# Second half of an attention and expert-layer kernel: new hand-written orders, chunk 0 normalised by VectorE, group scores from pair sums, both table reads ahead of the weight loads

## The chip, the cores and the metric

The kernel runs on one core of one Trainium2 chip. The metric is device microseconds (us) for one execution. The kernel before takes 311.48 us, the median of three runs (310.99 to 311.97).

Engines by the profile's names: PE is TensorE's matmul, PEld its weight load, DVE is VectorE, ACT ScalarE, POOL GpSimd, SP SyncE. SP only starts DMAs. Each engine works through its own list of instructions in order and waits on semaphores, so an instruction that waits holds up all that is behind it on its engine.

## The reference, cut to what matters

```
x = x + L0_xattn(layernorm(x), ctx)     # one head over 32 keys: softmax(qk)v, (x_norm + attended) Wo
x = x + L0_ffn(layernorm(x))            # 8 experts, top 1, gelu
x = x + L1_xattn(layernorm(x), ctx)     # 16 heads of 8 channels
x = x + L1_ffn(layernorm(x))            # 16 experts of 96, top 4, and one shared expert
```

`x` is (4, 512, 128). The routing of the last layer:

```
scores = sigmoid(x @ gate_w.T); sb = scores + gate_bias
group_scores = sum of the two largest sb in each of 4 groups of 4 experts
keep the 2 best groups, then the 4 best experts in them; w = 2.5 * score / sum
y = sum over experts of w * (silu(x w1) * (x w3)) w2 + shared expert
```

## The kernel before, in words

The 2048 tokens are four chunks (0 to 3) of 512, each of 4 tiles of 128 tokens. The first half (first attention, first expert layer) ends by writing its results to DRAM in sorted order. The second half fetches them back token by token (`fetch`, 16 indirect DMAs that POOL issues), adds them to `x` (`combine`), and does the second attention and the last expert layer.

The second half is one list of stages per engine, `ORDER1`, written out by hand, each entry `stage:number`. Up to `gturn` and the routing, numbers are chunks. For `g`, `u`, `e`, `prod`, `hm`, `high`, `low`, `silu` and `y` they are tiles of work: 52 of them, 13 a chunk, 12 routed row blocks (16 experts of 96 rows are 12 blocks of 128) and one shared.

A chunk's attention runs: statistics (DVE), `rstd2` (POOL: `ve`, `nm`, a power to `rstd`, a product to `shift_of`, lines 770 to 775), `norm2` (ACT, `normalise`, line 581), `turn2` (PE transposes, 1178), `unturn2` (ACT copy, 586), `q` (PE), `qcopy` (ACT), `score` (PE), `max` (DVE, four reductions of one bank each, 1037), `mturn` (PE transposes, 1373), `mcopy` (ACT), `scoreT` (PE), `exp` (ACT), `zav` (PE: sums into bank 4, products into bank 5), `div` (DVE: two reciprocals, 1045, 3.4 us together, then two products, 1051), `wo` (PE), `add` (DVE, 1056, with the statistics of the next normalisation). Then `rstd3`, `norm3`, `turn3`, `unturn3`, `round` (ACT: high half of x), `lowx` (POOL: low half, 779), `logit` (PE), `lgcopy` and `sg` (ACT), `route0` to `route7` (DVE, 30-odd short instructions that each wait for the one before), `gturn` (PE transposes of the gates, 1414) and `gcopy` (ACT).

A tile of expert work runs: `g` and `u` (PE, three matmuls of 512 columns each), `silu` (ACT), `prod` (DVE, 1143), `e` (PE, one matmul that spreads the gates), `hm` (DVE, 1154), `high` (ACT, 746), `low` (POOL, 854), `y` (PE, three matmuls). `g` writes bank 0, `u` bank 1, `e` bank 3, one buffer each: `g:n` waits for `silu:n-1`, `u:n` for `prod:n-1`, `e` for the `hm` before it.

`FILL` puts matmuls that compute nothing, of 512 bfloat16 columns, ahead of a chunk-0 stage on PE.

In the first expert layer SP reads two small tables into registers: which expert each of 23 token tiles has (`tile_e`) and where its tokens lie (`tile_r`). It reads the first, starts the first five weight loads, reads the second, waits for the scatter of the tokens and for the zero padding, and starts the token loads.

## Time and profile before

| | us |
|---|---|
| median of three runs | 311.48 |
| the profiled execution | 313.38 |
| its span, first to last instruction | 311.6 |
| PE busy | 264.1 (85%) |
| DVE busy | 191.7 (62%) |
| ACT busy | 162.9 (52%) |
| POOL busy | 155.4 (50%) |

An engine's busy time is the sum of its instructions' durations. Matmul records overlap a little, so PE can look full. The granted clock of PE over the span is 0.919 of full speed; it is at half (1.2 of 2.4 GHz) in three stretches of the windows asked for, 26 to 36 us, 40 to 70 us and 108 to 114 us, and at or near full from 70 to 107 us and from 115 us on.

By the profile's timeline the second half begins at 98.5 us with the first fetch; chunk 0's `turn2` starts at 109.67, the first expert tile (`g:0`) at 143.87 and the last `y` at 306.11.

### The profile page before, as it was taken

The page shows a single profiled execution, that of the slowest core. Times are in us where ns is not written, and L with a number is a line of the kernel's source. Part 1 is how long each engine was busy: PE and PEld are TensorE (multiplying, and loading weights), DVE is VectorE, ACT ScalarE, POOL GpSimd, SP SyncE. Part 2 cuts the span into 40 slices and gives each one's busy share as a digit, 9 for nine tenths or more (in the row PEclk, how much of TensorE's full clock was granted, in tenths as well). Part 3 has the DMA queues.
Part 4 walks back from the last instruction along what each step waited for, and adds up shares of the span by engine and source line. Part 5 has one row for each costly group of instructions (what it writes and reads, how often), then busy time and mean ns, then how long its engine had stood idle before and what let it go on. Part 6 is the DMA issues. An engine that isn't in the chain of part 4 may idle for free. (4 is left out here: it accounts for less than half of the span.)

```text
span 311.6 us, 4963 instructions
## 1 busy us (share of the span) xinstructions
PE 264.1 (85%) x1542; PEld 193.6 (62%) x1542; DVE 191.7 (62%) x577; ACT 162.9 (52%) x324; POOL 155.4 (50%) x182
## 2 busy tenths in 40 slices
PE   8899962259989287979899987999899989899993
PEld 7689852249984042444468645875477867687871
DVE  5555557014441348666975998689976599665561
ACT  2946330485641034157488654878457745455541
POOL 6722577439402888251176151743178535565561
PEclk9996655559999969999999999999999999999998
DMA  7960013447841111000000000000000000000000
GB/s 239 405 236 1 18 35 101 119 127 191 241 130 37 51 35 34 8 2 0 2 0 2 1 0 1 2 0 14 23 1 0 2 34 1 1 2 34 0 0 34
DMA packets 15372, 16.86 MB, mean 54 GB/s; under 512 B 2147, under 2 KB 13011, under 8 KB 15091
## 3 DMA queue, kind: packets, MB, share of 16 engines
q1 hardware_dynamic: 9520, 11.65, 11.8%
q10 hardware_dynamic: 4802, 2.80, 2.9%
q0 software_dynamic: 1024, 2.10, 2.4%
q8 instruction: 12, 0.20, 0.3%
q14 instruction: 14, 0.11, 0.1%
HBM read 11.96 MB, written 4.59 MB: 53 GB/s over the span
## 5 line engine op out<-in xcount | busy, mean ns | idle before, releaser
L854 POOL TENSOR_TENSOR lring<-hm,hring 128x512 fp32r<-128x512 f32 (+1 forms) x52 | 67.9, 1307 | 77.6 <-ACT hring L746 76.3
L740 ACT ACTIVATE act<-bank 128x512 f32<-128x512 f32 (+1 forms) x52 | 31.0, 597 | 38.5 <-PE bank L1166 38.3
L1143 DVE TENSOR_TENSOR act<-act,bank 128x512 f32<-128x512 f32 x48 | 32.9, 685 | 27.0 <-PE bank L1166 25.7
L1166 PE MATMUL bank<-xTh,gu1h 128*128 128x512 f32 (+1 forms) x104 | 43.6, 419 | 2.6 <-DVE hm L1154 1.7
L1166 PE MATMUL bank<-xTh,gu1l 128*128 128x512 f32 (+1 forms) x104 | 41.1, 395 | 0.0
L1166 PE MATMUL bank<-xTl,gu1h 128*128 128x512 f32 (+1 forms) x104 | 40.8, 393 | 0.0
L581 ACT ACTIVATE xn<-x,shift_of,rstd 128x128 f32<-128x128 f32 x64 | 26.4, 483 | 26.4 <-POOL shift_of L775 26.3
L1154 DVE TENSOR_TENSOR hm<-act,bank 128x512 f32<-128x512 f32 (+1 forms) x52 | 35.6, 685 | 7.4 <-PE bank L1166 4.9
L746 ACT CAST hring<-hm 128x512 fp32r<-128x512 f32 (+1 forms) x52 | 32.1, 618 | 12.4 <-DVE hm L1154 11.4
L1166 PEld LDWEIGHTS bank<-xTh,gu1h 128*128 128x128 f32 (+1 forms) x104 | 19.3, 186 | 14.8 <-DVE act L1143 3.6
L788 POOL DMA_INDIRECT xn<-sorted_y,home x16 | 15.7, 983 | 21.2 <-DMA sorted_y<-ys 17.3
L1166 PE MATMUL bank<-hring,w2h 128*128 128x512 f32 (+1 forms) x52 | 21.6, 414 | 1.7 <-POOL lring L854 1.7
L1166 PEld LDWEIGHTS bank<-xTh,gu1l 128*128 128x128 f32 (+1 forms) x104 | 19.3, 186 | 4.8
L1166 PE MATMUL bank<-warm_b,onesb 128*128 128x512 bf16 x87 | 21.2, 391 | 0.5 <-issue 0.5
L1166 PEld LDWEIGHTS bank<-xTl,gu1h 128*128 128x128 f32 (+1 forms) x104 | 19.4, 186 | 3.3
L1178 PE MATMUL bank<-pack_a,xn 128*128 128x128 f32 x64 | 12.8, 315 | 9.3 <-ACT xn L581 8.1
L1166 PE MATMUL bank<-lring,w2h 128*128 128x512 f32 (+1 forms) x52 | 20.5, 395 | 0.0
L1166 PE MATMUL bank<-hring,w2l 128*128 128x512 f32 (+1 forms) x52 | 20.5, 395 | 0.0
L1166 PE MATMUL bank<-gT,sel 128*128 128x512 f32 x48 | 19.9, 414 | 0.6 <-DVE hm L1154 0.6
L682 ACT ACTIVATE hT<-bank,w 128x128 f32<-128x128 f32 x46 | 14.4, 364 | 10.5 <-PE bank L1166 10.5
L784 POOL DMA_INDIRECT sorted_x<-xn,slot x16 | 15.8, 985 | 4.6 <-issue 4.6
L586 ACT COPY xT<-bank 128x512 f32<-128x512 f32 x16 | 9.4, 584 | 16.0 <-PE bank L1178 13.2
(217 smaller groups left out, 521.0 us busy)
## 6 DMA issues: line engine op xcount, KB each, us to landing
w<-in_w SPq DMA_DIRECT2D x23, 129.0 KB, 2.4
wf<-in_gu SPq DMA_DIRECT2D x1, 1632.0 KB, 14.2
xs<-sorted_x SPq DMA_DIRECT2D x23, 64.0 KB, 2.5
sorted_y<-ys ACTq DMA_DIRECT2D x11, 128.0 KB, 3.1
x<-in_x SPq DMA_DIRECT2D x4, 256.0 KB, 5.1
w<-in_w SPq DMA_DIRECT2D x1, 1024.0 KB, 9.6
out_x<-x SPq DMA_DIRECT2D x4, 256.0 KB, 2.0
w<-in_w SPq DMA_DIRECT2D x1, 768.0 KB, 14.9
```

The costliest lines, as they stand in the source:

```text
L581: nc.scalar.activation(normal(k, b)[:, j, :], x[:, b * TPB + j, :], ACT.Identity, bias=shift_of[:, ln(k, b), j:j + 1], scale=rstd[:, ln(k, ...
L586: nc.scalar.copy(xT[:, xT_slot(k, b), :], bank[n][:, :]).then_inc(s.xT_ready[k], 1)
L682: last = nc.scalar.activation(hT0[:, t % 2, k, :], bank[2 + t % 2][:, k * P:(k + 1) * P], ACT.Gelu, bias=b1_tile[:, t % SLOTS0, k:k + 1])
L740: nc.scalar.activation(act[0:m, n % 4, :], bank[0][0:m, :], ACT.Silu).then_inc(s.act_ready1, 1)
L746: nc.scalar.copy(hring[0:m, n % 4, :], hm[0:m, n % 4, :]).then_inc(s.hmh_ready, 1)
L784: nc.gpsimd.indirect_dma_start(xs_dram[:, :], bass.IndirectOffsetOnAxis(ap=slot0[:, t:t + 1], axis=0), xn2[:, t, :], None).then_inc(s.scat ...
L788: nc.gpsimd.indirect_dma_start(xn2[:, t, :], None, ys_dram[:, :], bass.IndirectOffsetOnAxis(ap=home0[:, t:t + 1], axis=0))\
L854: nc.gpsimd.tensor_tensor(lring[0:m, n % 4, :], hm[0:m, n % 4, :], hring[0:m, n % 4, :].bitcast(F32), ALU.subtract).then_inc(s.hml_ready, 1)
L1143: nc.vector.tensor_tensor(act[:, n % 4, :], act[:, n % 4, :], bank[1][:, :], ALU.mult).then_inc(s.prod_ready1, 1)
L1154: nc.vector.tensor_tensor(hm[0:m, n % 4, :], act[0:m, n % 4, :], bank[1 if r == SHARED[c] else 3][0:m, :], ALU.mult).then_inc(s.hm_ready1, 1)
L1166: return nc.tensor.matmul(dst, lhsT, rhs, start=start, stop=stop, skip_group_check=True)
L1178: last = nc.tensor.transpose(quarters(n)[:, j, :], normal(k, b)[:, j, :], ident)
```

## The change

Five things change.

1. `ORDER1` has new orders on all four engines. `max` is now entered four times a chunk, a bank each (`max:4c` to `max:4c+3`), and the two reciprocals of `div` are entries of their own (`recip:2c`, `recip:2c+1`), so that `prod` and `hm` can stand between them. The statistics are entries of their own too (`stat2`, `stat3`). `mturn` waits for all four maxima as before, and each product of `div` for its own reciprocal.
2. Chunk 0's two normalisations in the second half (`norm2:0`, `norm3:0`) move from ACT to DVE, as four `tensor_scalar` each (subtract the mean, multiply by `rstd`). POOL then computes no `nm` and no `shift_of` for them.
3. `route1` takes the largest of the six sums of pairs in a group of four, instead of max and min of pairs: four instructions in place of seven.
4. SP reads both tables before it starts the five weight loads.
5. `FILL` goes from q 4, mturn 8, turn3 14, logit 2 to q 1, mturn 7, turn3 6, logit 1; score, scoreT, zav (2 each) and wo (13) stay.

```diff
-        "combine:0 combine:1 max:0 combine:2 div:0 combine:3 add:0 max:1 route0:0 route1:0 ...
+        "combine:0 norm2:0 max:0 max:1 max:2 max:3 combine:1 stat2:1 combine:2 recip:0 recip:1 div:0 add:0 "
...
-        "fetch:10 fetch:11 rstd2:1 fetch:12 fetch:13 bias1:1 fetch:14 rstd2:2 fetch:15 rstd2:3 rstd3:0 bias1:2 "
+        "fetch:10 fetch:11 fetch:12 rstd2:1 rstd3:0 fetch:13 lowx:0 bias1:1 fetch:14 rstd2:2 fetch:15 low:0 "
...
-FILL = {"q": 4, "score": 2, "mturn": 8, "scoreT": 2, "zav": 2, "wo": 13, "turn3": 14, "logit": 2}
+FILL = {"q": 1, "score": 2, "mturn": 7, "scoreT": 2, "zav": 2, "wo": 13, "turn3": 6, "logit": 1}
...
-            for t in range(LEAD0):
-                load_weights(t, experts[t])
             sp.wait_ge(s.table_ready, 2)
             _, first = nc.values_load_multi_w_load_instructions(
...
+            for t in range(LEAD0):
+                load_weights(t, experts[t])
...
+                if k >= 2 and b == 0:
+                    nc.gpsimd.tensor_scalar(ve[:, own, :], mv[:, own, :, 1], EPS, None, ALU.add).then_inc(s.ln_step[k], 3)
+                    pool.wait_ge(s.ln_step[k], 3)
+                    nc.gpsimd.tensor_tensor(rstd[:, own, :], ve[:, own, :], mhalf[:, 0:TPB], ALU.pow).then_inc(s.ln_rstd[k], 1)
+                    return
...
+            def invert(c, h):
+                v.wait_ge(s.av_mm, 2 * c + 1)
+                nc.vector.reciprocal(half(rz1, h), half(bank[4], h)).then_inc(s.rz1_ready, 1)
...
+            def normalise_first(k):
+                own = ln(k, 0)
+                v.wait_ge(s.ln_rstd[k], 1)
+                for j in range(TPB):
+                    nc.vector.tensor_scalar(normal(k, 0)[:, j, :], x[:, j, :], mv[:, own, j, 0:1], rstd[:, own, j:j + 1],
+                                            ALU.subtract, ALU.mult).then_inc(s.xn_ready[k], 1)
...
+                    four = sbs[:, t, :].rearrange("p t (g w) -> p (t g) w", g=NG)
+                    sums = pair[:, t0 * NG:t1 * NG, :]
+                    nc.vector.tensor_tensor(sums[:, :, 0:3], four[:, :, 0:3], four[:, :, 1:4], ALU.add)
+                    nc.vector.tensor_tensor(sums[:, :, 3:5], four[:, :, 0:2], four[:, :, 2:4], ALU.add)
+                    step(nc.vector.tensor_tensor(sums[:, :, 5:6], four[:, :, 0:1], four[:, :, 3:4], ALU.add))
+                    step(nc.vector.tensor_reduce(gs[:, t, :].rearrange("p t g -> p (t g)"), sums, AX, ALU.max))
```

Three places show how the instructions move. The first is DVE at the start of the second half. `x<-xn,score,x x4` is a `combine`, `mpad<-bank` the maxima, `rz` and `aT` the division, `x<-x,bank` the `add`, and `xn<-x,mv,rstd` the new normalisation. Before:

```order
L880 BN_AGGR mv<-st 128x2 x4
L1037 TENSOR_REDUCE mpad<-bank 128x4x4 x4
L1020 SCALAR_TENSOR_TENSOR x<-xn,score,x 128x128 x4
L873 BN_STATS st<-x 128x6 x4
L880 BN_AGGR mv<-st 128x2 x4
L1045 RECIPROCAL rz<-bank 128x256 x2
L1051 TENSOR_TENSOR aT<-bank,rz 128x256 x2
L1020 SCALAR_TENSOR_TENSOR x<-xn,score,x 128x128 x4
L873 BN_STATS st<-x 128x6 x4
L880 BN_AGGR mv<-st 128x2 x4
L1056 TENSOR_TENSOR x<-x,bank 128x512
```

After, the same stretch:

```order
L1065 TENSOR_SCALAR xn<-x,mv,rstd 128x128 x4
L1043 TENSOR_REDUCE mpad<-bank 128x4x4 x4
L1027 SCALAR_TENSOR_TENSOR x<-xn,score,x 128x128 x4
L880 BN_STATS st<-x 128x6 x4
L887 BN_AGGR mv<-st 128x2 x4
L1027 SCALAR_TENSOR_TENSOR x<-xn,score,x 128x128 x4
L1051 RECIPROCAL rz<-bank 128x256 x2
L1059 TENSOR_TENSOR aT<-bank,rz 128x256 x2
L1071 TENSOR_TENSOR x<-x,bank 128x512
```

The normalisation stands ahead of chunk 0's maxima, chunk 1's `combine` behind them, and nothing stands between the division and the `add`; chunk 3's `combine` has gone far back, behind `prod:5`.

The second is PE ahead of the first expert tile. `xn1` transposed is `turn3:0`, `mpad` transposed is `mturn:1`, `R1w,xT` is `logit:0`, `warm_b` are the fills. Before:

```order
L1166 MATMUL bank0<-warm_b,onesb 128x512 x14
L1178 MATMUL bank3<-pack_a,xn1 128x128 x4
L1373 MATMUL bank4<-pack_a,mpad 128x128 x4
L1166 MATMUL bank0<-warm_b,onesb 128x512 x2
L1166 MATMUL bank2<-R1w,xT 128x128 x4
L1166 MATMUL bank4<-qT,Kd 128x512
```

After:

```order
L1185 MATMUL bank0<-warm_b,onesb 128x512 x6
L1197 MATMUL bank3<-pack_a,xn1 128x128 x4
L1185 MATMUL bank0<-warm_b,onesb 128x512
L1185 MATMUL bank2<-R1w,xT 128x128 x4
L1392 MATMUL bank4<-pack_a,mpad 128x128 x4
L1185 MATMUL bank4<-qT,Kd 128x512
```

Nine fills go, and `logit:0` stands ahead of `mturn:1`.

The third is DVE at the division of chunk 2 (`act<-act,bank` is `prod`, `hm<-act,bank` is `hm`). Before:

```order
L1045 RECIPROCAL rz<-bank 128x256 x2
L1051 TENSOR_TENSOR aT<-bank,rz 128x256 x2
L1143 TENSOR_TENSOR act<-act,bank 128x512
L1154 TENSOR_TENSOR hm<-act,bank 128x512
L1143 TENSOR_TENSOR act<-act,bank 128x512
L1056 TENSOR_TENSOR x<-x,bank 128x512
```

After:

```order
L1051 RECIPROCAL rz<-bank 128x256
L1162 TENSOR_TENSOR act<-act,bank 128x512
L1051 RECIPROCAL rz<-bank 128x256
L1059 TENSOR_TENSOR aT<-bank,rz 128x256 x2
L1162 TENSOR_TENSOR act<-act,bank 128x512
L1173 TENSOR_TENSOR hm<-act,bank 128x512
L1071 TENSOR_TENSOR x<-x,bank 128x512
```

A `prod` now stands between the two reciprocals.

## Rows read from the trace of the kernel before

**Rows 1.** Windows: busy time (and instructions) of PE, PEld, DVE, ACT, POOL, clock, DMA
```profile
240.00:260.00 20.00, 18.66 (x86) 14.49 (x85) 15.40 (x43) 11.80 (x20) 8.74 (x7) 1.00 0.04 14
280.00:300.00 20.00, 20.00 (x90) 16.04 (x89) 11.58 (x17) 10.79 (x18) 10.83 (x9) 1.00 0.03 13
```

**Rows 2.** PE timeline, waits of over 1 us: start, duration, operation [idle before <-releaser]
```profile
190.19 0.61 PE L1414 MATMUL bank<-pack_a,gate 128*32 128x128 f32 x4 [2.25 <-DVE aT L1051]
...
224.60 0.61 PE L1414 MATMUL bank<-pack_a,gate 128*32 128x128 f32 x4 [1.20 <-DVE aT L1051]
...
252.95 0.50 PE L1166 MATMUL bank<-xTh,gu1h 128*128 128x512 f32 x1 [1.34 <-DVE hm L1154]
...
266.16 0.60 PE L1414 MATMUL bank<-pack_a,gate 128*32 128x128 f32 x4 [1.11 <-DVE gate L1122]
...
306.11 0.50 PE L1166 MATMUL bank<-hring,w2h 128*128 128x512 f32 x1 [1.33 <-POOL lring L854]
```

**Rows 3.** POOL timeline, the start of chunk 0
```profile
106.13 0.95 POOL L788 DMA_INDIRECT xn<-sorted_y,home  x1 [0.30 <-issue]
107.14 0.24 POOL L770 TENSOR_SCALAR ve<-mv 128x4 f32<-128x4 f32 x1
...
107.77 1.05 POOL L773 TENSOR_TENSOR rstd<-ve,mhalf 128x4 f32<-128x4 f32 x1
```

**Rows 4.** ACT timeline, the start of chunk 0
```profile
109.13 1.65 ACT L581 ACTIVATE xn<-x,shift_of,rstd 128x128 f32<-128x128 f32 x4 [13.20 <-POOL shift_of L775]
111.35 0.59 ACT L586 COPY xT<-bank 128x512 f32<-128x512 f32 x1 [0.57 <-PE bank L1178]
```

**Rows 5.** PE timeline, the start of chunk 0
```profile
109.67 1.64 PE L1178 MATMUL bank<-pack_a,xn 128*128 128x128 f32 x4 [6.75 <-ACT xn L581]
111.10 1.91 PE L1166 MATMUL bank<-warm_b,onesb 128*128 128x512 bf16 x4
112.81 1.88 PE L1166 MATMUL bank<-xT,pack_b 128*128 128x512 f32 x2
```

**Rows 6.** DVE timeline: a tensor_scalar, chunk 0's statistics, a combine, an add, maxima
```profile
6.04 0.27 DVE L935 TENSOR_SCALAR bqrep<-ones,pack_a 128x128 f32<-128x128 f32 x1
...
105.70 0.38 DVE L880 BATCH_NORM_AGGREGATE mv<-st 128x2 f32<-128x6 f32 x4
...
131.01 1.13 DVE L1020 SCALAR_TENSOR_TENSOR x<-xn,score,x 128x128 f32<-128x128 f32 x4
...
133.38 0.65 DVE L1056 TENSOR_TENSOR x<-x,bank 128x512 f32<-128x512 f32 x1
...
136.63 2.48 DVE L1037 TENSOR_REDUCE mpad<-bank 128x16 f32<-128x512 f32 x4 [1.28 <-PE bank L1166]
```

**Rows 7.** PE timeline from chunk 0's wo to the first expert tile
```profile
130.82 1.16 PE L1166 MATMUL bank<-pack_b,aT 128*128 128x128 f32 x8
...
135.27 0.40 PE L1166 MATMUL bank<-maskrow,onesb 32*128 32x512 bf16 x4 [1.00 <-ACT qT L702]
...
136.49 3.19 PE L1166 MATMUL bank<-warm_b,onesb 128*128 128x512 bf16 x14
...
143.87 0.48 PE L1166 MATMUL bank<-xTh,gu1h 128*96 128x512 f32 x1
```

**Rows 8.** Windows, the same columns, PE idle at the start of chunk 0
```profile
108.00:109.00 1.00, 0.00 (x0) 0.00 (x0) 0.00 (x0) 0.00 (x0) 0.92 (x2) 0.50 0.03 8
```

**Rows 9.** DVE timeline, two routing instructions of the same size
```profile
175.89 1.36 DVE L1086 TENSOR_TENSOR route<-gs 128x64 f32<-128x64 f32 x1
177.17 0.21 DVE L1087 TENSOR_TENSOR route<-gs 128x64 f32<-128x64 f32 x1
```

**Rows 10.** POOL timeline at the same time
```profile
175.87 1.29 POOL L854 TENSOR_TENSOR lring<-hm,hring 128x512 fp32r<-128x512 f32 x1 [6.94 <-ACT hring L746]
```

**Rows 11.** SP timeline, the first weight and token loads
```profile
54.11 7.43 SPq L533 DMA_DIRECT2D w<-in_w  x5
63.66 2.40 SPq L539 DMA_DIRECT2D xs<-sorted_x  x5
```

56 lines of the change are left out of this document (25 added, 31 removed), and 81 rows, old and new, of the table ORDER1.

## The prediction

> **What bounds the kernel now.** I read the windows first, then PE's own timeline with the waits it names, then the timelines of the engines that release it. The windows show two different regimes. From 280 to 300 us PE is busy for all 20.00 us with 90 matmuls, 0.22 us each, while DVE, ACT and POOL are busy a little over half of it; from 240 to 260 us PE is busy for 18.66 us and DVE for 15.40 [rows 1]. So from the first expert tile on PE is the bound, and what can be won there is only the time in which it waits. PE's timeline says where the long waits are: 2.25, 1.20, 1.34 and 1.11 us, three of them in front of a gate transpose (two released by the products of a division, one by the last routing instruction), one in front of a `g` or `u` released by an `hm`, all by DVE, and one of 1.33 us in front of the last `y`, released by POOL at the end of the chain prod, hm, high, low [rows 2]. Together the four are 5.90 us. A matmul's record runs past the start of the next one, so each wait cost some 0.1 to 0.2 us more than it reads.
>
> The second regime is ahead of the first expert tile, up to 143.87 us. There every engine waits for the one before it, on chunk 0's chain; a microsecond off that chain is a microsecond off the end, as long as PE has its work in order behind it. The chain shows as POOL's `rstd` work [rows 3], ACT's four normalisations [rows 4], and PE's transposes, fills and `q` [rows 5].
>
> **Start of chunk 0 (changes 2 and 5).** The statistics are done at 105.70 + 0.38 = 106.08 us [rows 6]. POOL starts `ve` only at 107.14, since fetch 6 (0.95 us) stands ahead of it, and ACT starts at 109.13 [rows 3, 4]. After, `rstd2:0` stands ahead of fetch 6: `ve` at about 106.15, 0.24 us, then the power, 1.05 us [rows 3], with 0.07 us between; DVE can start at 107.6. That is 1.5 us earlier. The four normalisations take ACT 1.65 us [rows 4]. A `tensor_scalar` of this size on DVE took 0.27 us alone [rows 6], so four take between half of 1.1 us (pipelined) and 1.1 us; I take 0.9. PE's four transposes took 1.64 us [rows 5], paced by ACT and at half clock: the granted clock was 0.50 from 108 to 109 us [rows 8], the low level of 1.2 GHz, after PE had stood idle for 6.75 us before 109.67 [rows 5]. I leave them at the low level: they end about 109.5 in place of 111.31, 1.8 us earlier. The copy `unturn2` ends at 111.35 + 0.59 = 111.94 [rows 4], yet `q` starts at 112.81, behind four fills that began at 111.10 [rows 5]. With one fill `q` starts at the copy's end, 0.8 us sooner. Sum 1.8 + 0.8 = 2.6 us at `q`. From `q` to `wo:0` the same instructions follow each other in both versions, each on an engine that is free, so I carry 2.6 us to `wo:0`. DVE's `combine:1` (1.13 us undisturbed [rows 6]) now comes behind the maxima and lies in the wait for `mcopy`, `scoreT`, `exp` and `zav`.
>
> Here a rule speaks against the change. In the trace a `tensor_tensor` of 64 elements a partition took 1.36 us when POOL's `low`, 175.87 to 177.16, was under way, and its twin behind it 0.21 us [rows 9, 10]: DVE stood still until POOL was done, 1.15 us. The Trainium skill, SBUF — State Buffer, "Who interferes with whom", calls this an exclusive lock on a port pair that VectorE and GpSimd share, and counts `tensor_scalar` and DMAs issued by GpSimd among those that meet on it; by that rule the trace agrees for `low`, and whether a normalisation meets fetch 6, which POOL starts in the same moment, no row shows. If one waits out fetch 6, 0.95 us [rows 3], this term is 1.6 us. Its bounds are 1.6 and 3.0 us, the upper one with the short normalisation.
>
> **From wo:0 to the first expert tile.** Before, this takes 143.87 − 130.82 = 13.05 us [rows 7]. `score:1` starts 4.45 us after `wo:0` [rows 7], 1.00 of it in wait for `qcopy`; ACT's order no longer has `norm2:2` ahead of `qcopy:1`, worth 0.4. Then 14 fills take 3.19 us [rows 7], 0.23 each; six take 1.4, so 1.8 us go. Is `norm3:0` ready by then? `wo:0` ends near 129.4 on the new clock; `add` (0.65 [rows 6]) follows at once, where before `combine:3` stood between, statistics 1.25, POOL 1.36 (`ve` and the power), the normalisation 0.9: 133.7. PE's last fill ends near 134.8, so PE's list decides and not the data. What comes late next is the order logit, mturn: `mturn:1` now waits for `unturn3` and `logit:0`, 0.6 + 0.6 us, instead of going first, and DVE's maxima (2.48 us [rows 6]) fit into that time. The stretch gives 0.4 + 1.8 − 1.2 = 1.0 us. `g:0` starts 3.6 us earlier, at about 140.3.
>
> **The routing of chunk 0.** This is the place that the new order makes worse. `hm:0` stands behind all eight routing pieces and `gturn:0` ahead of `u:1`; before, `hm:0` stood behind six and `gturn:0` came much later. And POOL now has `lowx:0`, `bias1:1` and `rstd2:2` in those same 7 us (they follow `fetch:13` in its list), while before, the last two were done ahead of the routing. Each can hold a routing instruction as rows 9 and 10 show, up to 1.15 us. Against that, PE no longer stands before a division three stages later. I give back 0.9 us of the 3.6, with bounds of 0 and 3.5 (three times 1.15). After this point 2.7 us are left.
>
> **Chunks 1 to 3 (change 1).** The wait of 2.25 us is in front of `gturn:1`, behind both reciprocals and the products; after, `gturn:1` comes a tile and a half later in PE's list and a `prod` stands between the reciprocals. But DVE has to do the same work in that stretch: from `prod:8` to the products of the division it has seven prod or hm of 512 elements at 0.65 (as the `add` of rows 6), some 25 routing instructions of 0.21 and a gap of 0.05 [rows 9], two reciprocals of 3.4 us together and the products, 0.7: 15 us. PE has thirteen groups of three matmuls and four `e` at 0.22 each [rows 1], and 3.8 for `scoreT` and `zav`: 13.5 us. So about 1.0 of the 2.25 comes back as waits in front of `u:12` and `wo:2`; 1.25 go. In chunk 2 the pieces are spread over five more groups of matmuls, 3.3 us, and PE's stretch is no longer the shorter one, so the 1.20 go. In chunk 3 `hm:30` now stands ahead of the routing and not behind two pieces of it, and `gturn:3` three tiles later: 1.34 and 1.11 go. Sum 4.9 us. The bounds are 0, if each wait only moves, and 5.9, all four.
>
> **Tail.** `y:48` now stands behind `e:51`, so the last `hm` starts three matmuls of 0.22 us earlier [rows 1], and the wait before the last `y` was 1.33 [rows 2]: 0.7 us.
>
> **Unseen.** About 400 entries move, and each place where a wait was priced at nothing may have one. I subtract 1.0 us.
>
> **Both tables first (change 4).** On SP the five weight loads take 7.43 us from 54.11, then the second table is read until the token loads start at 63.66, 2.1 us [rows 11]. The order of the two on one queue changes nothing in the sum. But the same queue starts five token loads in 2.40 us [rows 11], so the weight loads are slowed by what runs beside them, and 2.1 us later less runs there. I take 1.0 us, bounds 0 and 2.1; the weights come later, but the tokens they are for come last in any case.
>
> **Pair sums (change 3).** Three instructions fewer of 0.1 to 0.2 us, 0.4 us of DVE a chunk. I cost them at nothing on their own: they lie inside the stretches above.
>
> **Sum.** 2.7 + 4.9 + 0.7 − 1.0 + 1.0 = 8.3 us. The profiled execution took 313.38 us with a span of 311.6, 1.9 above the median of 311.48; the profile after should show 305.1, and the median 303.2.
>
> **The rivals.**
>
> *Only the head start stays.* The waits of chunks 1 to 3 move and do not go, since DVE's list is as long as before. For it: DVE is busy 15.40 of 20 us there [rows 1]. Against it: the maxima and reciprocals no longer come as blocks of 2.5 and 3.4 us. Gain 2.7 + 1.0 = 3.7, time 307.8. Chance 0.23.
>
> *Everything fits.* No port hit in chunk 0's routing (3.6), all four waits (5.9), the tail (0.7), the tables in full (2.1), and 1.5 us of shorter waits that the rows do not list. 13.8 us, time 297.7. Chance 0.13.
>
> *POOL holds DVE, chunk after chunk.* The new DVE lists put routing pieces singly behind a `prod`, when POOL is in `low`, 1.29 us of each tile [rows 10]; before, most lay behind an `hm` or in a lump. A hit costs 1.15 us [rows 9]. Chunks 1 to 3 have seven pieces each so placed or near it; DVE has 4.6 us of slack in 20 [rows 1], so the mechanism decides from the fourth additional hit in a chunk. With five additional hits in each of four chunks, 23 us, and half of that on PE's path, 11.5 us, the 8.3 become −3.2 and the time is 314.7, slower than before. The page named above states this lock as a rule, which is why it has a chance of its own: 0.09.
>
> *The clock falls in chunk 0's routing.* The waits only change places, and PE's wait before `gturn:0` grows past 4 us, with the clock falling as it did in the idle time before 109.67 [rows 5, 8]. The expert matmuls behind it then take twice their 0.22 us, 3.7 us more if that lasts for 17 of them, and the gain of 3.7 is spent: 311.5, within 0.3%. Chance 0.05.
>
> **How the numbers follow.** The forecast has 0.50. Measurement tells 0.3%, 0.9 us, from no change. The forecast, the first rival and the second are faster: 0.86. The fourth rival is no change: 0.05. The third is slower: 0.09. The range of the forecast's own case adds the bounds of its terms: 300.5 to 306.5. To hold 8 in 10 it goes to 298.0 below, most of the way to the second rival, and to 309.0 above, past the first.
>
> **What would show it.** `turn2:0` 1.8 us and `q:0` 2.6 us earlier against the last fetch-bound statistics; `g:0` 3.6 us earlier against the same mark; POOL's `lowx` and `bias1:1` beside long routing instructions, and a PE wait before `gturn:0` or `u:1`; the waits of rows 2 gone except one near `u:12` or `wo:2`; token loads started at 62.7 or before. The prediction is wrong if the clock falls inside chunk 0's routing, if the token loads start no earlier, or if new waits of over 1 us in chunks 1 to 3 add up to more than 2 us.

## The result, and the profile after

The changed kernel took 323.18 us in the median of its first four executions (318.99 to 327.08), the kernel before 311.24 beside it: ratio 1.026, 95% interval 1.021 to 1.031, slower. I had forecast 303.2 us in a range of 298.0 to 309.0. The profiled execution took 318.99 us, with a span of 317.2.

Two of the four executions took 327.08 and 326.61 us and were not profiled, so where they spent 8 us more than the profiled one is not known.

Later series gave a different size for the same kernel: 310.56 us beside 311.05 for before, 317.73 beside 315.29 (1.013, 1.006 to 1.021), 312.61 beside 309.36 (1.015, 0.986 to 1.044). Ratios are made of the executions without a visibly lower clock; medians are made of all. The table below the profile breaks the profiled executions into stretches, which repeat far more exactly than the medians do.

POOL and VectorE at the start of chunk 0, in the first profile after (they answer to [rows 3, 6]):
```profile
105.19 0.24 POOL L773 TENSOR_SCALAR ve<-mv 128x4 f32<-128x4 f32 x1 [0.40 <-issue]
105.51 1.04 POOL L775 TENSOR_TENSOR rstd<-ve,mhalf 128x4 f32<-128x4 f32 x1
106.75 1.15 POOL L795 DMA_INDIRECT xn<-sorted_y,home  x1 [0.20 <-issue]
...
115.64 0.94 POOL L795 DMA_INDIRECT xn<-sorted_y,home  x1 [0.30 <-issue]
```
```profile
106.59 1.33 DVE L1065 TENSOR_SCALAR xn<-x,mv,rstd 128x128 f32<-128x128 f32 x4 [1.55 <-POOL rstd L775]
117.78 2.48 DVE L1043 TENSOR_REDUCE mpad<-bank 128x16 f32<-128x512 f32 x4 [9.86 <-remote]
```
TensorE in the same profile, from the transposes to the first expert tile and the gate transposes (for [rows 5, 7]):
```profile
106.99 1.31 PE L1197 MATMUL bank<-pack_a,xn 128*128 128x128 f32 x4 [2.99 <-DVE xn L1065]
...
108.98 2.07 PE L1185 MATMUL bank<-xT,pack_b 128*128 128x512 f32 x2 [0.46 <-ACT xT L588]
...
112.13 1.07 PE L1185 MATMUL bank<-Kd,qT 32*128 32x128 f32 x32
113.37 1.46 PE L1185 MATMUL bank<-warm_b,onesb 128*128 128x512 bf16 x6 [0.16 <-issue]
120.32 1.12 PE L1392 MATMUL bank<-pack_a,mpad 128*128 128x128 f32 x4 [5.50 <-DVE mpad L1043]
...
145.63 0.44 PE L1185 MATMUL bank<-xTh,gu1h 128*96 128x512 f32 x1
...
152.82 1.01 PE L1433 MATMUL bank<-pack_a,gate 128*32 128x128 f32 x4 [1.82 <-DVE gate L1131]
```
Up to the score matmuls, done at 112.13 + 1.07 = 113.20 us, the start is as forecast. Then VectorE does not begin its first maximum for 4.58 us; this is called the stand below. The view names no releaser ("remote"). The trace also keeps the time at which each semaphore rose: the one that this maximum waits for, and that the last score matmul sets, rose at 117.76 us, 4.55 us after that matmul and 0.02 us ahead of the maximum. So VectorE went on at once when it was told; it was told late. TensorE runs out of fills and stands 5.50 us, and the windows show what that does to its clock (stretch, PE busy (instructions), granted clock, DMA):
```profile
116.00:118.00 2.00, 0.00 (x0) 1.00 0.26 66
118.00:120.00 2.00, 0.00 (x0) 0.67 0.00 0
120.00:122.00 2.00, 1.68 (x6) 0.50 0.00 0
122.00:124.00 2.00, 2.00 (x9) 0.50 0.00 0
```
SP's loads, for [rows 11]: the five weight loads took 5.26 us here, and the token loads start 3.6 us earlier than in the profile before.
```profile
54.60 5.26 SPq L535 DMA_DIRECT2D w<-in_w  x5
60.11 2.40 SPq L541 DMA_DIRECT2D xs<-sorted_x  x5
```

**All profiles by stretch.** "Fetch to g:0" runs from POOL's first row fetch to the first expert tile, "g:0 to end" from there to the end of the span. "At 1.2 GHz" is an estimate of the time lost to the low clock behind g:0: time x (1 - granted clock), summed up to the last matmul, since the clock also falls at the end, where TensorE has nothing left. "Held" counts VectorE instructions, from 8 us ahead of g:0 on, that took over 0.3 us more than the quickest of the same line and form, and sums the excess. Times in us.

```
run            first fetch  fetch to g:0  g:0 to end  at 1.2 GHz  held          median, before beside it
before            98.51        45.36        167.73       0.0       6:  5.5 us   311.48
before2           95.28        45.32        167.70       0.0       6:  5.5      312.76, 315.29
tables_only      101.62        44.80        167.68       0.0       6:  5.5      312.98, 311.05
pairs_only        94.17        44.80        167.53       1.6       7:  6.0      307.77, 308.99
after (first)     97.49        48.14 stand  171.57       1.7      19: 17.4      323.18, 311.24
again             96.00        41.71        171.69       1.7      19: 17.5      310.56, 311.05
again2           100.52        47.25 stand  170.83       1.7      19: 17.5      317.73, 315.29
again3            95.97        41.76        171.67       1.7      19: 17.5      312.61, 309.36
tables_back       93.47        42.01        171.82       1.7      19: 17.5      309.82, 311.05
more_fills        94.54        44.78        171.78       1.7      19: 17.5      312.58, 311.05
gturn_late        94.57        41.47        170.96       1.7      19: 17.5      310.03, 308.99
fill_gturn        95.25        41.54        171.01       1.7      19: 17.5      312.75, 309.47
bias_early        96.13        41.56        171.81       5.1      18: 16.3      311.40, 308.99
expert_first      92.92        41.86        174.72       5.1      17: 16.7      311.32, 309.47
combined          93.75        42.57        171.98       3.4      16: 15.5      309.78, 309.47
start_only        91.79        42.47        175.24       5.1       9:  8.0      312.20, 308.99
start_only2       95.15        41.52        171.53       2.4      11:  9.0      308.89, 309.47
best2             92.54        47.13 stand  169.23       1.4      10:  7.9      318.13, 315.29
fetch_split       93.53        48.72        171.85       1.7      19: 17.5      315.96, 309.36
combine_first     93.27        41.87        171.76       1.7      19: 17.5      312.43, 309.36
```
Three readings. First, ahead of the first fetch the same program varies by several us from execution to execution (91.8 to 100.5 in kernels that differ only behind it), so no edit there can be judged by one profile. Second, the new start shortens the stretch to g:0 from 44.8 or 45.3 us to 41.5 to 42.6, except where VectorE stands and where an edit adds work or a wait there (more_fills, fetch_split). Third, the new order makes the stretch behind g:0 longer by 4.0 us, alike to 0.3 us in the seven profiles whose clock falls at the same place.

The ratios of the later kernels, with their intervals: gturn_late 1.009 (1.002 to 1.015), bias_early 1.014 (0.994 to 1.033), expert_first 1.004 (0.999 to 1.008), combined 1.001 (0.996 to 1.006), start_only 1.015 (0.999 to 1.031), fetch_split 1.032 (1.013 to 1.051), combine_first 1.016 (0.991 to 1.041). No kernel with the new start is shown to be faster than the one before.

### The profile page after: what moved, and what is told of

The parts are those of the page before. It is cut to its first block, busy times and chain, and to the rows that moved or that the text cites. A ratio compares the mean times of both kernels' runs of the same rounds, so it can differ in the third digit from the quotient of the medians.

```text
span 317.2 us, 4920 instructions
## 1 busy us (share of the span) xinstructions
PE 265.0 (84%) x1525; PEld 195.0 (61%) x1529; DVE 200.9 (63%) x573; ACT 158.0 (50%) x316; POOL 154.3 (49%) x178
## 4 chain that ended last, share of the span: by engine, by line
PE 46%; DVE 21%; issue 11%; POOL 7%; ACT 7%; another core or an unknown queue 3%; ACTq 2%; DMA 2%; POOLq 1%; DVEq 0%
PE bank L1185 41%; POOL lring L861 4%; DVE act L1162 2%; ACTq L650 2%; DVE hm L1173 2%; DVE mpad L1043 2%; PE bank L1197 2%; POOL xn L795 2%; DMA x<-in_x 1%; ACT xT L588 1%; ACT xn L583 1%; ACT gu1h L657 1%; DVE route L1112 1%; DVE route L1111 1%
## 5 line engine op out<-in xcount | busy, mean ns | idle before, releaser
L1185 PE MATMUL bank<-xTh,gu1h 128*128 128x512 f32 (+1 forms) x104 | 45.0, 433 | 4.2 <-DVE act L1162 3.5
L1185 PE MATMUL bank<-xTh,gu1l 128*128 128x512 f32 (+1 forms) x104 | 41.5, 399 | 0.0
L1162 DVE TENSOR_TENSOR act<-act,bank 128x512 f32<-128x512 f32 x48 | 32.7, 682 | 12.5 <-PE bank L1185 11.1
L583 ACT ACTIVATE xn<-x,shift_of,rstd 128x128 f32<-128x128 f32 x56 | 23.1, 484 | 7.8 <-POOL shift_of L782 7.5
L1185 PE MATMUL bank<-w,hT 128*128 x92 | 16.3, 305 | 3.3 <-ACT hT L684 3.2
L1011 DVE TENSOR_TENSOR ys<-bank,b 128x128 f32<-128x128 f32 x23 | 6.7, 292 | 19.5 <-PE bank L1185 19.5
L1185 PE MATMUL bank<-warm_b,onesb 128*128 128x512 bf16 x70 | 17.7, 394 | 1.1 <-issue 1.1
```

What stands on the lines that cost most here:

```text
L583: nc.scalar.activation(normal(k, b)[:, j, :], x[:, b * TPB + j, :], ACT.Identity, bias=shift_of[:, ln(k, b), j:j + 1], scale=rstd[:, ln(k, ...
L1011: nc.vector.tensor_tensor(ys[:, u % (2 * PAIRS0), :], bank[4 + u % 2][:, 0:C], b2_0[:, bass.ds(own_expert[u], 1), :].rearrange("p o c -> p ...
L1162: nc.vector.tensor_tensor(act[:, n % 4, :], act[:, n % 4, :], bank[1][:, :], ALU.mult).then_inc(s.prod_ready1, 1)
L1185: return nc.tensor.matmul(dst, lhsT, rhs, start=start, stop=stop, skip_group_check=True)
```

## Experiments

**Does the stand recur? again, and the clock: more_fills.** The first is the changed kernel unedited; the second:
```diff
-FILL = {..., "mturn": 7, ...}
+FILL = {..., "mturn": 27, ...}
```


> The changed kernel as it is, profiled a second time. Theory P (the hold belongs to the program: something at this place of VectorE's list or of its surroundings holds it each time): VectorE's first maximum of chunk 0 again starts some 4 us after the last score matmul (117.8 against 113.2 in the first profile) and TensorE again idles over 5 us there. Theory O (one execution's accident): the maximum starts within 0.7 us of the last score matmul, as in the kernel before (0.6), and the span is 3 to 5 us shorter than 317.2, at 312 to 314 us.

> The changed kernel with 27 in place of 7 warm matmuls ahead of the first transposes of the maxima, so that TensorE is busy from 113.4 to about 118.3 us or later. Theory C (a good part of what is lost at the start of chunk 0 is the clock that falls to 0.50 when TensorE idles 5.5 us, about 2 us from the transposes of the maxima to the output projection): if the hold is there, the granted clock stays at or above 0.9 from 114 to 133 us and the projection comes 1.5 to 2.5 us earlier after the transposes (10.8 us in place of 12.9). Theory D (VectorE's hold alone decides, the clock is made good elsewhere): the kernel's time changes by under 0.5 us. If the hold is not there, the fills themselves cost up to 4 us.

VectorE and TensorE of again:
```profile
105.02 1.33 DVE L1065 TENSOR_SCALAR xn<-x,mv,rstd 128x128 f32<-128x128 f32 x4 [1.55 <-POOL rstd L775]
112.04 2.48 DVE L1043 TENSOR_REDUCE mpad<-bank 128x16 f32<-128x512 f32 x4 [5.69 <-PE bank L1185]
```
```profile
137.71 0.44 PE L1185 MATMUL bank<-xTh,gu1h 128*96 128x512 f32 x1
```
This profile is as theory O says at the maximum, which starts 0.07 us behind the score. Fetch to g:0 is 41.71 us, 6.4 less than in the first profile, and the span is 309.4, under the 312 to 314 of the theory, since the first fetch also came 1.5 us earlier. Of the 6.4, 4.5 are the stand and 1.7 its clock (5.1 us lost between fetch and g:0 in place of 3.4). That it is one execution's accident does not hold: the stand came again, in best2 and again2 below. With no stand to cover, the 27 fills of more_fills only cost their own time: 44.78, 3.1 more. Whether they would keep the clock up in a stand was not seen.

**The tables: tables_back and tables_only.** The order of the two groups on SP, undone in the new kernel and done in the old one:
```diff
 tables_back
+            for t in range(LEAD0):
+                load_weights(t, experts[t])
             sp.wait_ge(s.table_ready, 2)
             _, first = ...
-            for t in range(LEAD0):
-                load_weights(t, experts[t])
```


> The changed kernel with the five weight loads put back between the two table loads. Theory T (starting the token loads 3.6 us earlier costs time, since TensorE starts its layer at 62.7 us, then waits 3.0 us for ScalarE and stays at the 1.2 GHz level to 74 us): 1 to 1.5 us faster than the changed kernel. Theory F (what I predicted, that both tables first is worth 1.0 us): 1.0 us slower than the changed kernel. If the hold of VectorE ahead of the first maximum depends on when POOL's fetches run, which this edit shifts by about 1 us, the hold changes too; if it belongs to the program, it stays near 4 us.

> The kernel before with only the order of the table loads changed (both tables ahead of the five weight loads). Theory T: 0.5 to 1.5 us slower than the kernel before (312 to 313 us), with TensorE's layer starting near 62.7 us and its granted clock low until 74 us. Theory F: 0.5 to 1.5 us faster (310 to 311 us). The start of chunk 0 and all behind it keep their distances from the first fetch in both.

Neither theory can be told from the other: the first fetch came at 93.47 us with the weight loads first and at 96.00 with the tables first (again); in the old kernel at 98.51 and 95.28 against 101.62. SP's lines in tables_back, and then the five weight loads in the second profiles of the kernel before and of the changed one, before2 and again2:
```profile
54.51 2.44 SPq L535 DMA_DIRECT2D w<-in_w  x5
60.26 2.40 SPq L541 DMA_DIRECT2D xs<-sorted_x  x5
```
```profile
51.29 7.41 SPq L533 DMA_DIRECT2D w<-in_w  x5
```
```profile
55.98 5.30 SPq L535 DMA_DIRECT2D w<-in_w  x5
```
The five weight loads took 2.44 us in all four profiles of this series, before or behind the table, so here there was nothing to win by taking them out of the way. In before2 the 7.43 of [rows 11] came back as 7.41, and behind both tables the loads took 5.26, 5.30 and 5.83 us (after, again2, best2). So in those two series they were shorter by 1.6 to 2.2 us with the tables first, yet the first fetch shows no clear gain: 98.51 and 95.28 us with the old order, 97.49, 100.52 and 92.54 with the new.

**The old order behind g:0: start_only, start_only2, best2.** The three have the new start and then the lists of before; combine:3, the statistics of chunks 2 and 3 and their layer norms had to be placed anew (in start_only2 and best2 ACT's norm2:3 also stands behind silu:5):
```diff
 start_only (PE; the other three lists in the same way)
-... zav:1 g:1 gturn:0 u:1 g:2 e:1 u:2 ...
+... zav:1 g:1 u:1 g:2 y:0 turn2:2 wo:1 q:2 gturn:0 u:2 ...
 start_only (POOL)  ... low:0 bias1:2 rstd3:1 rstd2:3 low:1 bias1:3 low:2 ...
 start_only2 (POOL) ... low:0 bias1:2 rstd3:1 low:1 low:2 rstd2:3 low:3 low:4 bias1:3 ...
 best2: as start_only2, with bias1:1 behind rstd2:1
```


> The changed kernel, with the kernel before's order of everything behind the first expert tile g:0 (chunks 1 to 3, their routing, statistics and layer norms), the new start of chunk 0 kept. Theory O (the new order of chunks 1 to 3 lets POOL hold VectorE's small routing instructions at 19 places, 17.4 us in all, against 6 places and 5.5 us before, and that makes the stretch from g:0 to the end 171.7 us instead of 167.7): the stretch is back at 167 to 169 us with 8 holds or fewer, while fetch to g:0 stays at 41.7 us; 3 to 4 us faster than the changed kernel. Theory S (the longer stretch comes with chunk 0's earlier start or its new routing, whatever order follows): the stretch stays above 170.5 us.

> As the run with the kernel before's order behind g:0, which had a wait of 3.8 us that my own placing of rstd2:3 ahead of low:1 on POOL made (and 1.2 GHz for 7 us behind it); here rstd2:3 stands behind low:2, bias1:3 behind low:4, norm2:3 behind silu:5. Theory O (the order of chunks 1 to 3 is what lengthened the stretch from g:0 to the end): no wait above 2.3 us, 9 holds or fewer of VectorE, and the stretch at 167 to 168.5 us less what the clock takes (1.7 us for each stretch at 1.2 GHz). Theory S (chunk 0's start or its routing does it): 170 us or more with the clock's share taken off.

> The new start with the kernel before's order behind g:0 (as in the second run of that kind), and POOL's bias1:1 behind rstd2:1, so that it holds VectorE no longer in chunk 0's routing (L1087 0.2 us for 1.3). If a hold taken away ahead of a late gate counts: the wait for hm at g:0 + 6.4 us (1.04) or for aT at + 10.3 (0.83) goes, the stretch g:0 to end is 1 us shorter than 171.5 at the same clock losses (2.9 us), 169 to 170.5 us, and the median is 1 to 3 us under before's. If not, the stretch stays at 171 us or more and the kernel equals before within 1 us.

start_only made a wait of its own. POOL's `rstd2:3` waits for statistics, and `low:1`, queued behind it, is what the next `y` needs:
```profile
153.69 0.23 POOL L776 TENSOR_SCALAR ve<-mv 128x4 f32<-128x4 f32 x1 [3.06 <-DVE mv L886]
...
155.57 1.26 POOL L860 TENSOR_TENSOR lring<-hm,hring 128x512 fp32r<-128x512 f32 x1
```
```profile
156.89 0.80 PE L1184 MATMUL bank<-hring,w2h 128*128 128x512 f32 x1 [3.83 <-POOL lring L860]
```
It tests nothing but shows the price of such an entry, 3.83 us and 1.2 GHz behind it. start_only2 without it: 11 holds for 19, 171.53 us with 2.4 us at 1.2 GHz, so 169.1 without the clock's share, against 167.7 for before and 170.0 for again by the same subtraction. That lies between the bounds of theory O (168.5) and theory S (170). best2: 10 holds, 169.23 and 1.4, so 167.8. So the direction is theory O's: of 2.3 us between again and before, start_only2 gives back 0.9 and best2, which also moves `bias1:1`, 2.2. The subtraction is an estimate, since a matmul that would have waited anyway loses nothing by the low clock, and as measured best2 is still 1.5 us longer than before. These kernels change the places of all engines behind g:0 together, so they show that the order lengthened the stretch and not that the holds alone did. Neither is faster than before: start_only2 308.89 beside 309.47 (0.997, 0.992 to 1.002), best2 318.13 beside 315.29 (1.003, 0.995 to 1.011), with the stand in its profile.

**What a hold costs: bias_early and expert_first.**
```diff
 bias_early (POOL)
-... fetch:12 rstd2:1 rstd3:0 fetch:13 lowx:0 bias1:1 fetch:14 ...
+... fetch:12 rstd2:1 bias1:1 rstd3:0 fetch:13 lowx:0 fetch:14 ...
 expert_first (DVE)
-... hm:8 route2:1 route3:1 prod:9 route4:1 hm:9 ...   -... route3:2 route4:2 prod:20 hm:19 ...
+... hm:8 prod:9 route2:1 route3:1 hm:9 route4:1 ...   +... route3:2 hm:19 route4:2 prod:20 ...
```


> The changed kernel with POOL's bias1:1 (1.3 us) moved from behind lowx:0, where it holds VectorE's L1088 for 1.1 us in chunk 0's routing, to behind rstd2:1, where VectorE waits anyway. Theory H (a hold moves the gate one for one): L1088 takes 0.2 us in place of 1.3, the gate transposes come 1.1 us earlier, TensorE waits 0.7 us there and its clock stays at 1.00; the stretch g:0 to end is 170.6 (the hold alone) to 169.1 us (with the clock). Theory V (another small instruction meets POOL's next one in its place): L1088 is quick but the next ones are held, and the gate comes as late as before.

> The changed kernel with three of VectorE's places changed: prod:9 ahead of route2:1 (it stood behind route3:1), hm:9 one routing piece earlier, hm:19 ahead of route4:2 (it stood behind it and prod:20). POOL's order is untouched. Theory Q (a hold costs only what TensorE waits for behind it): there are still 17 to 19 holds of 16 to 17.5 us in all, but the waits at g:0 + 39 us (1.91) and + 80 us (2.12) go or fall under 0.5 us, and the stretch is 2.5 to 4 us shorter than 171.7. Theory R (VectorE's total work decides, whatever its order): the waits come back at the next tiles and the stretch changes by under 1 us.

In bias_early the instruction behind the held one is quick (1.32 us in again):
```profile
136.32 1.29 DVE L1086 TENSOR_TENSOR pair<-sbs 128x32 f32<-128x32 f32 x1
137.52 0.17 DVE L1087 TENSOR_TENSOR pair<-sbs 128x16 f32<-128x16 f32 x1
```
```profile
143.81 0.60 PE L1432 MATMUL bank<-pack_a,gate 128*32 128x128 f32 x4 [0.75 <-DVE gate L1130]
```
The gate wait falls by 1.07, as theory H says, and the later waits of 1.56 and 1.20 us go too or fall to 0.44: TensorE's waits behind g:0 sum to 10.5 us in place of 13.6. Yet the stretch is 171.81, where theory H had 169.1 to 170.6. Its clock now fell twice, from 175 us on and here to 223 us, 5.1 us in all:
```profile
214.00:216.00 2.00, 0.46 (x2) 1.00 0.01 4
216.00:218.00 2.00, 2.00 (x7) 0.60 0.04 8
218.00:220.00 2.00, 1.56 (x6) 0.50 0.00 0
```
expert_first went against theory Q. The 1.91 us wait did go, but the next one, 1.56 us in again, grew, with 1.2 GHz behind it:
```profile
181.10 0.79 PE L1184 MATMUL bank<-gT,sel 128*128 128x512 f32 x1 [3.69 <-DVE hm L1172]
```
16.7 us of holds stayed, and TensorE's waits even grew by 0.8. The waits came back at the next tiles, as theory R says, but the stretch became 3.0 us longer, which neither theory had; 3.4 us more are spent at the low clock.

**The wait before the gate transposes and its clock: gturn_late and fill_gturn.**
```diff
 gturn_late (PE; on DVE hm:0 ahead of route6:0)
-... zav:1 g:1 gturn:0 u:1 g:2 e:1 ...
+... zav:1 g:1 u:1 g:2 gturn:0 e:1 ...
 fill_gturn
-FILL = {..., "logit": 1}
+FILL = {..., "logit": 1, "gturn": 8}      (these fills write bank 3)
```


> The changed kernel with chunk 0's gate transposes moved on TensorE behind u:1 and g:2 (and hm:0 on VectorE ahead of route6:0, which u:1 needs). TensorE no longer stands 1.8 us before them. Theory K (the wait and the clock that falls to 0.66 behind it, 7 matmuls at 0.43 us each instead of 0.23, together cost 3.3 of the 4.0 us): the stretch g:0 to end falls from 171.7 to 168.4 us, with a granted clock of 1.00 right through. Theory L (the later waits of 0.8 to 2.1 us take over, since VectorE is as late as before): it falls by less than 1.5 us.

> The changed kernel with 8 warm matmuls (1.9 us at 2.4 GHz) ahead of chunk 0's gate transposes, where TensorE otherwise stands 1.8 us; VectorE's holds and the gate's time are unchanged. Theory C (the 1.2 GHz stretch behind this wait costs 1.7 us by itself): granted clock 1.00 from g:0 + 6 to g:0 + 12 us, the stretch g:0 to end 170.0 us (169.8 to 170.3). Theory N (the tiles there wait for VectorE anyway): 171.3 us or more.

Both keep the clock at 1.00 at the gate transposes, where in again it is:
```profile
144.00:146.00 2.00, 1.11 (x5) 0.76 0.08 21
146.00:148.00 2.00, 2.00 (x6) 0.50 0.00 0
```
and both gain only 0.7 us, since the clock fell at the wait 79 us behind g:0 instead. TensorE's row of fill_gturn there, and its windows:
```profile
215.80 0.79 PE L1185 MATMUL bank<-gT,sel 128*128 128x512 f32 x1 [2.12 <-DVE hm L1173]
```
```profile
214.00:216.00 2.00, 0.20 (x1) 0.95 0.01 4
216.00:218.00 2.00, 2.00 (x5) 0.50 0.00 0
218.00:220.00 2.00, 2.00 (x12) 0.70 0.00 0
```
The same wait of 2.12 us left the clock at 1.00 in again (214 to 218 us). So theory C is right for the place and wrong for the sum, which neither theory had.

**The routing's own change: pairs_only.** The kernel before with piece 1 as four pair-sum instructions:
```diff
-  (seven tensor_tensor: max/min of pairs, of quarters, their sum)
+  nc.vector.tensor_tensor(sums[:, :, 0:3], four[:, :, 0:3], four[:, :, 1:4], ALU.add)
+  nc.vector.tensor_tensor(sums[:, :, 3:5], four[:, :, 0:2], four[:, :, 2:4], ALU.add)
+  step(nc.vector.tensor_tensor(sums[:, :, 5:6], four[:, :, 0:1], four[:, :, 3:4], ALU.add))
+  step(nc.vector.tensor_reduce(gs..., sums, AX, ALU.max))
```


> The kernel before with only piece 1 of the routing changed to pair sums. Theory Z (what I predicted, no effect on the whole): 0.3 us either way, the stretch g:0 to end at 167.5 to 168.0 us, the holds of VectorE at other lines but not more than 7. Theory P (the pair sums are themselves what POOL holds): more holds in piece 1, 8 or more in all, and the stretch 1 us or more longer.

Theory Z: 167.53 us, 7 holds, ratio 1.000 (0.993 to 1.008). Its waits behind g:0 sum to 9.9 us against 11.1, the one of 1.34 us in [rows 2] is gone, and 1.6 us at 1.2 GHz came instead, from 300 us on.

**All edits together: combined.** bias_early, gturn_late and expert_first in one.

> The changed kernel with bias1:1 on POOL behind rstd2:1, gturn:0 on TensorE behind g:2 with hm:0 ahead of route6:0 on VectorE, and the three places of VectorE changed as in the run of those alone. If the stretch behind g:0 is a sum of waits behind holds and of stretches at 1.2 GHz, it comes to 164 to 166.5 us (before 167.7), with fetch to g:0 at 40 to 41.7 us: 4 to 6 us faster than the kernel before in executions with the same clock, so 303 to 305 us in the median of a series in which before has 309. If waits come back at other tiles, the stretch is 168 us or more and the kernel equals the one before within 1.5 us.

171.98 us with 3.4 at 1.2 GHz, median 309.78 beside 309.47. The sum I expected did not come: the 3.69 us wait of expert_first is in it.

**The stand: again2, before2, again3, fetch_split, combine_first.** The first three are the two kernels unedited. The others:
```diff
 fetch_split, combine_first (POOL)
-... fetch:8 fetch:9 fetch:10 fetch:11 fetch:12 rstd2:1 rstd3:0 ...
+... fetch:8 fetch:9 rstd2:1 fetch:10 fetch:11 fetch:12 rstd3:0 ...
 combine_first (DVE)
-norm2:0 max:0 max:1 max:2 max:3 combine:1 stat2:1 combine:2 ...
+norm2:0 combine:1 stat2:1 max:0 max:1 max:2 max:3 combine:2 ...
```


> The changed kernel as it is, a third profile and a longer series. Theory A (its own effect is 3.3 to 3.6 us less ahead of g:0 and 4.0 us more behind it; the stand of VectorE ahead of the first maximum is not the program's): fetch to g:0 41.5 to 42.1 us, g:0 to end 171.5 to 171.9, VectorE's first maximum under 0.7 us behind the last score matmul, and a median within 2 us of before's. Theory B (the first result is its time: 2.6% slower): a median of 316 us or more beside 309 of before, and the stand of 3 us or more in this profile too.

> The kernel before as it is, a second profile and a longer series. Theory A: fetch to g:0 44.8 to 45.4 us and g:0 to end 167.5 to 167.9 us again (less or more by 1.7 where the clock falls at another place); the first fetch anywhere between 93 and 102 us, since the stretch ahead of it varies from execution to execution in both kernels. Theory B: the same, but with a median 6 us or more below that of the changed kernel beside it.

> The changed kernel once more, beside the two kernels below. If the stand belongs to a series of executions, this profile shows whether this is one: first maximum 3.2 to 4.6 us behind the last score matmul (fetch to g:0 47 to 48 us), or 0.07 us (41.5 to 42.1 us). g:0 to end 170 to 172 us in both cases.

> The changed kernel with POOL's rstd2:1 moved from behind fetch:12 to behind fetch:9: only two fetches follow bias1:0 before POOL waits for VectorE's statistics. Theory F (VectorE stands until the rows of POOL's run of fetches have landed): where again3 shows the stand, here VectorE goes on about 1.1 us after the end of fetch:9, which is before the score is done, so no stand; fetch:10 and later come after the maxima, and combine:2 waits for them: fetch to g:0 42 to 44 us. Theory G (the stand has nothing to do with the fetches): it stays 3 us or more where again3 shows it.

> The changed kernel with VectorE's combine:1 and stat2:1 ahead of the maxima, as in the kernel before, and POOL's rstd2:1 behind fetch:9. Theory F: as above, the maxima start at once behind the score or behind stat2:1, whichever is later (0.1 to 0.6 us), fetch to g:0 41.5 to 42.5 us, and no stand even where again3 shows one. Theory G: the maxima, or combine:1 instead, stand 3 us or more where again3 shows it.

The stand came again in again2 and in best2, which ran in one series:
```profile
120.68 2.48 DVE L1043 TENSOR_REDUCE mpad<-bank 128x16 f32<-128x512 f32 x4 [9.74 <-remote]
```
```profile
118.66 0.95 POOL L795 DMA_INDIRECT xn<-sorted_y,home  x1 [0.30 <-issue]
```
It is in 3 of the 14 profiles with the new start as the change has it, 3.3 to 4.6 us each. All three times VectorE went on 1.07 to 1.20 us after POOL's fifth fetch in a row had ended (here 119.61 and 120.68). The semaphore times of the traces put these profiles in their place (times in us; the semaphore is the one that the score matmuls of chunk 0 set and the maxima wait for):

```
profile        score done  POOL's last fetch done  semaphore rose  late by  five weight loads
before            116.84         116.52                117.42        0.58        7.43
before2           113.58         113.27                114.14        0.57        7.41
after             113.21         116.58                117.76        4.55        5.26
again2            117.38         119.61                120.65        3.27        5.30
best2             108.99         111.62                112.70        3.71        5.83
the other 15         -              -                     -      0.04 to 0.05  2.44 to 2.47
```
So the kernel before has the late semaphore as well, in both of its profiles. Two things come together. One belongs to the series: all five profiles of two series (before and after; before2, again2 and best2) have it, with slow weight loads and fewer semaphore times in the trace (2972 to 3027 against 3445 to 3458), and none of the other 15 has, whatever their order; why is not known. The other belongs to the order: in these five the semaphore came 0.9 to 1.2 us after the end of POOL's run of fetches. With the old order that run ends 0.3 us ahead of the score, with the new one it goes on for 2.2 to 3.4 us behind it. Chunk 1's score fits: its semaphore was 0.80 to 0.83 us late in after, again2 and best2, where `fetch:13` runs beside it, and 0.05 to 0.06 in before and before2, where no fetch does. In the other 15 profiles fetches run beside a score too, and the semaphore is on time. That the fetches cause the delay is not shown: the two orders seen in such a series differ in much else.

again3 did not show the stand, so fetch_split and combine_first, run beside it, decide nothing on its cause. They do show prices: fetch_split makes `combine:2` wait for late rows, with the clock falling behind, 48.72 us; combine_first costs nothing (41.87) and leaves only 0.36 us between VectorE's work and the maximum.

Beside all executions of the kernel before in this series again2 is slower, 1.013 (1.006 to 1.021), and before2 is not, 1.000 (0.995 to 1.005). By its stretches theory A holds for before2 (45.32 and 167.70). again2 misses it on both sides: 170.83 us behind g:0, 0.7 under the range, and 47.25 ahead of it, 5.5 more than in again, by the stand and its clock. The two stretches together are 5.1 us longer than before2's, and the medians of the two are 5.0 apart (317.73 and 312.76).

## Why the prediction was wrong

*Start of chunk 0: right in its parts, with some luck in the sum.* Measured from the first fetch, `turn2:0` came 1.74 us earlier in again (forecast 1.8), `q:0` 2.74 (2.6), `wo:0` 3.0 and `g:0` 3.65 (3.6). The normalisation on VectorE took 1.33 us for 0.9 and did not wait out fetch 6, which ran beside it; the lower bound of that term was not needed. From `wo:0` to `g:0` 12.41 us against 13.05, 0.6 for 1.0. Luck lies in `wo:0` and `g:0`: the profile before carries the 0.57 us of its late semaphore and again does not. Against tables_only, which has the old order and no late semaphore, `wo:0` came 2.45 us earlier and `g:0` 3.1.

*The step that failed in the execution that was measured: "each on an engine that is free".* The step "From `q` to `wo:0` the same instructions follow each other in both versions" took no account of VectorE waiting for a score that was long done. This put 6.4 us into the first profile's 317.2. A sign stood in the trace of before, behind the last of [rows 5]: the maximum started 0.60 us behind chunk 0's score, at chunk 1 only 0.08 us. The new order puts a run of five fetches of POOL beside the score, where the old one has three that end ahead of its end. Why the semaphore is late at all, and in two series only, stays open.
```profile
115.77 1.07 PE L1166 MATMUL bank<-Kd,qT 32*128 32x128 f32 x32
```
```profile
117.44 2.48 DVE L1037 TENSOR_REDUCE mpad<-bank 128x16 f32<-128x512 f32 x4 [2.22 <-PE bank L1166]
```

*Chunks 1 to 3: the step that failed in every execution.* I wrote "some 25 routing instructions of 0.21 and a gap of 0.05", and from that "Sum 4.9 us" to be won. In again, chunk 1's routing ran like this on VectorE (the second, fourth and fifth of these are held: alone such instructions took 0.22, 0.17 and 0.22 us):
```profile
171.78 0.22 DVE L1097 TENSOR_TENSOR route<-route,pack_b 128x64 f32<-128x64 f32 x1
172.04 1.20 DVE L1098 TENSOR_TENSOR route<-route 128x64 f32<-128x64 f32 x1
173.27 0.22 DVE L1099 TENSOR_REDUCE gk<-route 128x16 f32<-128x64 f32 x1
173.53 0.92 DVE L1102 TENSOR_SCALAR gk<-gk 128x16 f32<-128x16 f32 x1
174.48 1.26 DVE L1103 TENSOR_TENSOR route<-sbs,gk 128x64 f32<-128x64 f32 x1
175.77 0.41 DVE L1107 MAX8 top<-route 128x8 f32<-128x16 f32 x4
176.21 0.69 DVE L1162 TENSOR_TENSOR act<-act,bank 128x512 f32<-128x512 f32 x1
```
with POOL beside it, and TensorE waiting for that last `act`:
```profile
171.81 2.60 POOL L861 TENSOR_TENSOR lring<-hm,hring 128x512 fp32r<-128x512 f32 x2 [5.79 <-ACT hring L748]
174.35 1.30 POOL L786 TENSOR_TENSOR xTl<-xT,xTh 128x512 fp32r<-128x512 f32 x1
```
```profile
176.95 0.50 PE L1185 MATMUL bank<-xTh,gu1h 128*128 128x512 f32 x1 [1.91 <-DVE act L1162]
182.96 0.50 PE L1185 MATMUL bank<-gT,sel 128*128 128x512 f32 x1 [1.56 <-DVE hm L1173]
...
217.42 0.50 PE L1185 MATMUL bank<-gT,sel 128*128 128x512 f32 x1 [2.12 <-DVE hm L1173]
...
220.51 0.51 PE L1185 MATMUL bank<-gT,sel 128*128 128x512 f32 x1 [1.20 <-DVE hm L1173]
```
Three small instructions are held for 2.8 us while POOL works without a gap, 19 of them for 17.5 us in the whole stretch, against 6 and 5.5 before. I had the price of one hold from [rows 9, 10] and used it in the rival and for chunk 0, but not for chunks 1 to 3 in the sum. TensorE's waits from chunk 1's routing to chunk 3's sum to 10.2 us in again and 7.2 before: 3.0 longer where I had 4.9 shorter. That is a miss of 7.9 us, and the whole miss behind g:0 is 7.7 (171.7 measured, 164.0 by my terms, 3.7 under 167.7). The rest balances: the tail gained 0.76 (0.7 forecast), chunk 0's routing cost 0.3 of waits, and the 1.5 that are then left of the 4.0 go to its clock (1.7 by the table), 1.8 for 0.9, and the 1.0 set aside for the unseen covers that. That holds stand ahead of these waits is shown; how much of the 3.0 is theirs and how much comes from the new places of the other instructions was not separated.

The Trainium skill, SBUF — State Buffer, "Who interferes with whom", says which instructions meet POOL on the shared ports: those with two SBUF inputs, and `tensor_scalar` and casts under conditions, never a reduce. The trace of again agrees: held were 15 of 68 `tensor_tensor` on SBUF and 4 of 20 `tensor_scalar`, and none of 16 reduces on SBUF, 16 MAX8 or 113 `tensor_tensor` that read a bank.

*The tables: not shown.* The weight loads did become 2.2 us shorter in the first pair of profiles (7.43 to 5.26) and the token loads started 3.6 us earlier in the profile, but the first fetch came only 1.0 us earlier, in a stretch that varies by 8.7 us among kernels that are alike up to there. That this is just the 1.0 of the term is luck.

*The rivals.* Nearest to what happened is "POOL holds DVE, chunk after chunk", which had 0.09. Its holds came, and its size was too large: 13 more holds in place of 20, 12.0 us in place of 23, and 2.5 us of net waits and 1.5 of clock in place of 11.5. The 4.0 less the head start of 3.1 to 3.65 is 0.4 to 0.9 us slower, not 3.2. In the first profile the stand came on top: it is 5.6 us longer than the profile before, 1.0 less ahead of the first fetch, 2.8 more up to g:0 and 3.8 more behind it. The fourth rival was right that the clock would fall in chunk 0's routing, and it took a wait of 1.82 us, not of 4. My own criterion, "if new waits of over 1 us in chunks 1 to 3 add up to more than 2 us", was met: 7.8 us in five waits (1.91, 1.56, 2.12, 1.20, 1.03). So was the clock falling in chunk 0's routing; the token loads did start earlier.

The difference of the first profile, 317.2 for 303.3 expected, is then 7.5 behind g:0, 6.4 between fetch and g:0, and nothing ahead of it (97.49 for 97.5, by luck).

## What to carry to other kernels

Price every small VectorE instruction that lands beside a POOL `tensor_tensor` at the held duration, not at its own, and count how many a new order puts there; here 19 were held, spread singly among expert work, and 6 in the old order. Before a term rests on the duration of a DMA issue, look at a profile from another series: 7.43 us came back as 7.41 in one series and was 2.44 in the others. Where a wait has an unnamed releaser, compare the end of the instruction that should have ended it. When an order is moved by hand, look for the entry that waits with something needed behind it: one on POOL cost 3.8 us and the clock.
